# First stage of a cross-attention and expert kernel: products from f16 halves, halves and norm rows on GpSimd, another order within a step

## What is computed

```python
x = x + _L0_xattn_ref(ctx_1024, _layernorm(x, axis=-1), w_q, w_kv, w_out, b_out)   # 16 heads of 16
x = x + _L0_ffn_ref(_layernorm(x, axis=-1), gate_w, gate_b, expert_w, expert_b)    # all 8 experts, weighted by top-2 counts
x = x + _L1_xattn_ref(_layernorm(x, axis=-1), ctx_1024, ctx_1024, mask)
x = x + _L1_ffn_ref(_layernorm(x, axis=-1), W1, b1, W2, b2, Wg, bg)                # top-2 routing
```

## Time and profile before

| | us |
|---|---|
| median of 3 executions | 1119.98 |
| the three | 1128.83, 1119.98, 1119.82 |
| profiled execution | 1129.09 |
| its span, first to last instruction | 1127.3 |
| busy in the span: TensorE | 1004.8 (89%) |
| VectorE | 788.8 (70%) |
| ScalarE | 545.1 (48%) |
| GpSimd | 448.9 (40%) |

### The profile page before, as it was taken

How to read it: one execution, slowest core, us unless ns; L and a number is a source line. 1 busy time by engine, 2 the same in 40 slices (tenths; PEclk the granted TensorE clock), 3 DMA queues, 4 the chain that set the end, 5 groups by cost and what they waited for, 6 DMA issues and landing times. The chain is left out here.

```text
span 1127.3 us, 30896 instructions
## 1 busy us (share of the span) xinstructions
PE 1004.8 (89%) x10536; PEld 709.5 (63%) x10536; DVE 788.8 (70%) x2287; ACT 545.1 (48%) x1087; POOL 448.9 (40%) x648
## 2 busy tenths in 40 slices
PE   3789999999999999987499999999987399999994
PEld 2456666666666666655256666666654288888873
DVE  4377777888777788874377888888875355666553
ACT  1266666666666666655214333334433054555541
POOL 5222222222222222200015666666665525555554
PEclk9699999999999999998699999999986599999998
DMA  4444344343434434310345555555552235555443
GB/s 124 129 125 128 109 127 122 112 128 112 123 115 121 127 109 126 99 59 3 115 145 152 170 180 181 176 178 167 172 175 87 95 83 89 99 97 97 82 70 44
DMA packets 104586, 133.92 MB, mean 119 GB/s; under 512 B 23680, under 2 KB 93776, under 8 KB 104272
## 3 DMA queue, kind: packets, MB, share of 16 engines
q1 hardware_dynamic: 90898, 113.86, 34.0%
q0 software_dynamic: 13536, 18.10, 9.1%
HBM read 93.78 MB, written 38.68 MB: 118 GB/s over the span
## 5 line engine op out<-in xcount | busy, mean ns | idle before, releaser
L631 DVE TENSOR_REDUCE smax<-psum 112x2 f32<-112x750 f32 x256 | 236.7, 936 | 59.3 <-PE psum L355 59.3
L539 ACT ACTIVATE probsT<-psum 125x896 f32<-125x896 f32 x192 | 175.9, 916 | 45.0 <-PE psum L370 44.9
L1487 POOL DMA_INDIRECT out_dram<-y,token_at x70 | 112.1, 1602 | 111.3 <-DMA out_dram<-y,token_at 56.2
L1568 ACT ACTIVATE h<-psum,b 128x256 f32<-128x256 f32 x140 | 58.7, 470 | 99.4 <-PE psum L1515 86.2
L390 PE MATMUL psum<-probsT,v_aug 125*32 125x112 f32 x3072 | 96.6, 268 | 0.0
L288 POOL TENSOR_SCALAR ln_var<-ln_mv 112x1 f32<-112x1 f32 x32 | 7.1, 221 | 208.3 <-DVE ln_mv L643 208.3
L296 POOL TENSOR_TENSOR ctx_lo<-ctxT,ctx_hi 128x750 f16<-128x750 f32 x32 | 51.5, 1611 | 90.6 <-ACT ctx_hi L546 90.6
L355 PE MATMUL psum<-k_stack,q_stack 63*128 63x375 f16 x512 | 84.5, 329 | 1.8 <-DVE smax L631 1.5
L1244 DVE SCALAR_TENSOR_TENSOR acc<-psum,neg_bias,acc 128x448 f32<-128x448 f32 x112 | 75.9, 680 | 11.4 <-PE psum L1063 10.9
L1039 POOL DMA_INDIRECT dispatch_dram<-rows,slots_at x64 | 64.1, 1002 | 46.7 <-DVE slots_at L1347 35.5
L370 PE MATMUL psum<-q_stack,k_stack 64*128 64x112 f16 x1536 | 71.0, 211 | 10.7 <-ACT probsT L539 7.6
(11 more groups left out here) (215 smaller groups left out, 2420.9 us busy)
## 6 DMA issues: line engine op xcount, KB each, us to landing
ctxT<-in_ctxT_dram SPq DMA_DIRECT2D x64, 375.0 KB, 3.7
k_stack<-k_hi_dram SPq DMA_DIRECT2D x64, 188.0 KB, 2.7
ctx_rows<-in_ctx_dram SPq DMA_DIRECT2D x32, 375.0 KB
rows_e<-dispatch_dram SPq DMA_DIRECT2D x70, 136.0 KB
w_raw<-in_w_dram SPq DMA_DIRECT2D x32, 256.0 KB
k_hi_dram<-k_hi SPq DMA_DIRECT2D x32, 188.0 KB, 2.1
k_lo_dram<-k_lo SPq DMA_DIRECT2D x32, 188.0 KB, 2.0
k_stack<-k_lo_dram SPq DMA_DIRECT2D x32, 188.0 KB, 2.8
```

What stands on the lines that cost most here:

```text
L539: nc.scalar.activation(probsT[:, p, c, hg, :, :, :].rearrange("p k h q -> p k (h q)"), psum[0:KC, 0:2, 0:4 * S], ACT.Exp, scale=float(HD) ...
L631: nc.vector.reduce_max(smax[:, (u - LAG_B) % 2, 2 * (s % 4) + s // 4::PAIRS], psum[0:S, pair_bank(s):pair_bank(s) + 2, 0:KV], AX.X).then_i ...
L1487: nc.gpsimd.indirect_dma_start(dram["out"], bass.IndirectOffsetOnAxis(token_at[:, n % 2, s:s + 1], 0), y[:, n % 2, s, :], None, compute_op ...
L1568: nc.scalar.activation(h[:, c, :], psum[:, 1 + c // 2, (c % 2) * TILE:(c % 2 + 1) * TILE], ACT.Relu, bias=b1[:, c, bass.ds(e, 1)]).then_in ...
```

## The change

It does six things, all in `attention_phase`:
1. The query product and the output product are made of f16 halves, three passes each. That needs halves of wq and wo (made once), and xnT_hi, xnT_lo and onT_hi, onT_lo per step: ScalarE writes the upper half from PSUM, VectorE subtracts it (xnT_lo, onT_lo).
2. ScalarE copies queries and keys from PSUM to SBUF once, in f32 (q_full, k_full, in the space of the early weights, called `early`). GpSimd makes q_hi, q_lo, k_hi, k_lo from there. TensorE waits for the copy only.
3. The norm rows xn and x1n are written by GpSimd.
4. On TensorE and ScalarE, `vals((0, 1))` of the new row come before the output product, scores 6 and 7 and `vals((2,))` before unit 4, and the sixth unit just before the queries; `values(2)` comes after the gate.
5. The upper halves of the weights are cast by ScalarE at the start.
6. Semaphores follow.

```diff
--- before.py
+++ after.py
-    wq = sb("wq", [128, DC, D], F32)
-    wk = sb("wk", [128, DC, D], F32)
+    early = sb("early", [128, 2, DC * D], F32)
+    wq, wk = (early[:, n, :].rearrange("p (c d) -> p c d", c=DC) for n in range(2))
+    after = early[:].rearrange("p n w -> p (n w)")
+    k_full = after[:, 0:DC * KV].rearrange("p (c n) -> p c n", c=DC)
+    q_full = after[:, DC * KV:DC * KV + DC * S].rearrange("p (c s) -> p c s", c=DC)
...
+            def ln1_rows_of(t, u):
+
+                xb = x_res[:, bass.ds(t * UNROLL + u, 1), :].rearrange("p o d -> p (o d)")
+                wait(pool, m["ln1_rs"], count(t, u, 1, 1))
+                wait(pool, m["xnT_done"], count(t, u - 1, 1, 1))
+                nc.gpsimd.tensor_scalar(xn[:], xb, ln1_mv[:, 0:1], ln1_rstd[:], ALU.subtract, ALU.mult).then_inc(m["xn_ready"], 1)
...
             ln1_rstd_of(0, 0)
+            ln1_rows_of(0, 0)
             ctx_low(0, 0)
...
+                if on[0]:
+                    wait(pool, m["qfull_ready"], count(t, u, 1, 1))
+                    wait(pool, m["q_out"], count(t, u - 2, 32, 32))
+                    nc.gpsimd.tensor_copy(q_hi[:, u % 2, :, 0:S], q_full[:]).then_inc(m["qhi_ready"], 1)
+                    wait(pool, m["qhi_ready"], count(t, u, 1, 1))
+                    nc.gpsimd.tensor_tensor(q_lo[:, u % 2, :, 0:S], q_full[:], q_hi[:, u % 2, :, 0:S], ALU.subtract).then_inc(m["qlo_ready"], 1)
                 if more:
                     ctx_low(t, u + 1)
+                if on[0]:
+                    for mc in range(DC):
+                        wait(pool, m["kfull_ready"], count(t, u, 2, mc + 1))
...
+                        nc.gpsimd.tensor_copy(k_hi[:, u % 2, mc, 0:KV], k_full[:, mc, :]).then_inc(m["khi_ready"], 1)
+                        wait(pool, m["khi_ready"], count(t, u, 2, mc + 1))
+                        nc.gpsimd.tensor_tensor(k_lo[:, u % 2, mc, 0:KV], k_full[:, mc, :], k_hi[:, u % 2, mc, 0:KV],
+                                                ALU.subtract).then_inc(m["klo_ready"], 1)
                 if more:
                     ln1_rstd_of(t, u + 1)
+                    ln1_rows_of(t, u + 1)
...
+                    wait(pool, m["x1nT_done"], count(t, u - LAG_D - 1, 1, 1))
+                    nc.gpsimd.tensor_scalar(x1n[:], x1, ln2_mv[:, 0:1], ln2_rstd[:], ALU.subtract, ALU.mult).then_inc(m["x1n_ready"], 1)
...
                         wait(pe, m["ctxlo_ready"], count(t, u, 1, 1))
-                        wait(pe, m["qlo_ready"], count(t, u, 1, 1))
+                        wait(pe, m["qfull_ready"], count(t, u, 1, 1))
                     else:
-                        wait(pe, m["klo_ready"], count(t, u, 2, 1))
+                        wait(pe, m["kfull_ready"], count(t, u, 2, 1))
...
+                if not a:
+                    last_unit()
...
                 if a:
+                    last_unit()
                     wait(pe, m["v_ready"], count(t, u - 1, 2, 1))
-                    wait(pe, m["xnT_ready"], count(t, u, 1, 1))
+                    wait(pe, m["xnTlo_ready"], count(t, u, 1, 1))
...
+                        for w, x in ((wq_hi, xnT_hi), (wq_hi, xnT_lo), (wq_lo, xnT_hi)):
...
                 pair_scores(0)
-                if d:
-                    values(2)
...
                 if d:
+                    values(2)
                     values(3)
...
                 pair_scores(5)
+                if a:
+                    vals((0, 1))
                 if d:
-                    wait(pe, m["onT_ready"], count(t, u - LAG_D, 1, 1))
-                    for kc in range(DC):
-                        last = nc.tensor.matmul(bank_d[0:S, 0:D], onT[:, kc, :], wo[:, kc, :], start=(kc == 0), stop=(kc == DC - 1))
+                    wait(pe, m["onTlo_ready"], count(t, u - LAG_D, 1, 1))
...
+                    for x, w in ((onT_hi, wo_hi), (onT_lo, wo_hi), (onT_hi, wo_lo)):
...
                 unit_scoresT(3)
-                if a:
-                    vals((0, 1))
                 pair_scores(6)
+                pair_scores(7)
+                if a:
+                    vals((2,))
                 unit_scoresT(4)
-                if a:
-                    vals((2,))
-                pair_scores(7)
...
+            nc.scalar.activation(wq_hi[:], wq[:], ACT.Copy).then_inc(m["weight_split"], 1)
+            act.wait_ge(m["wkv_in"], 32)
+            nc.scalar.activation(wk_hi[:], wk[:], ACT.Copy).then_inc(m["weight_split"], 1)
+            nc.scalar.activation(wv_hi[:], wv[:], ACT.Copy).then_inc(m["weight_split"], 1)
...
-                    if mc == 0:
-                        wait(act, m["k_out"], count(t, u - 2, 32, 32))
-                    nc.scalar.activation(k_hi[:, u % 2, mc, 0:KV], bank_a[:, 0:KV], ACT.Copy).then_inc(m["khi_ready"], 1)
+                    wait(act, m["klo_ready"], count(t, u - 1, 2, mc + 1))
+                    nc.scalar.activation(k_full[:, mc, :], bank_a[:, 0:KV], ACT.Copy).then_inc(m["kfull_ready"], 1)
...
+                if d and a:
+                    exps(t, u - LAG_D, 5)
...
                 unit_exp(2)
+                if a:
+                    vout((0, 1))
                 unit_exp(3)
                 if a:
-                    vout((0, 1))
+                    vout((2,))
                 unit_exp(4)
-                if a:
-                    vout((2,))
...
+                if a:
+                    wait(dve, m["xnT_ready"], count(t, u, 1, 1))
+                    wait(dve, m["q_done"], count(t, u - 1, 1, 1))
+                    nc.vector.tensor_tensor(xnT_lo[:, :, :].rearrange("p c s -> p (c s)"), psum[:, 3, 0:DC * S],
+                                            xnT_hi[:, :, :].rearrange("p c s -> p (c s)"), ALU.subtract).then_inc(m["xnTlo_ready"], 1)
...
-                klo(0)
...
                 pair_max(4)
-                klo(1)
+                if d:
+                    wait(dve, m["onT_ready"], count(t, u - LAG_D, 1, 1))
+                    wait(dve, m["out_done"], count(t, u - LAG_D - 1, 1, 1))
+                    nc.vector.tensor_tensor(onT_lo[:, :, :].rearrange("p c s -> p (c s)"), bank_d[:, 0:DC * S],
+                                            onT_hi[:, :, :].rearrange("p c s -> p (c s)"), ALU.subtract).then_inc(m["onTlo_ready"], 1)
...
-                if more:
-                    ln1_out(t, u + 1)
                 pair_max(7)
-                if d:
-                    wait(dve, m["ln2_rs"], count(t, u - LAG_D, 1, 1))
-                    wait(dve, m["x1nT_done"], count(t, u - LAG_D - 1, 1, 1))
-                    nc.vector.tensor_scalar(x1n[:], x1, ln2_mv[:, 0:1], ln2_rstd[:], ALU.subtract, ALU.mult).then_inc(m["x1n_ready"], 1)
```

More of the change, by code:

```diff
@@ L136, in attention_phase @@
     o_nat = sb("o_nat", [S, D], F32)
-    onT = sb("onT", [128, DC, S], F32)
+    onT_hi, onT_lo = sb("onT_hi", [128, DC, S], F16), sb("onT_lo", [128, DC, S], F16)
     ln2_stats = sb("ln2_stats", [S, 6], F32)
@@ L579, in step @@
                     negate_maxima()
-                if d:
+                if d and not a:
                     exps(t, u - LAG_D, 5)
```

98 lines of the change are left out of this document (54 added, 44 removed).

## The result

The changed kernel takes 1137.49 us (median of 4 executions, 1134.97 to 1142.01), the kernel before on the same chip 1124.4 us (1119.82 to 1131.87). The ratio is 1.0116, 95% interval 1.0075 to 1.0157. The forecast was 1088.9 us; the change is slower by about 1%.

A forecast was written before the change was run, and what follows sets the result against it. TensorE's row of instructions was taken to set the 15.13 us step. Savings less one new wait gave 1.04 us per step, 29.1 over 28 steps, plus 2 at the start: 31.1, so 1119.98 becomes 1088.9 us, range 1078 to 1108.

The forecast's parts named there:

- the price of xn and x1n on GpSimd: Norm rows written by GpSimd: 0.47 us each, in 4.8 us of added GpSimd work per step, 8.8 in all.
- the new wait for maximum 6: TensorE's transposes of xn need the bank that maximum 6 on VectorE still uses: 0.15 us lost per step.
- Query product, 0.27: TensorE's query product as twelve f16 passes takes 0.72 us instead of 0.99: 0.27 saved per step, bounds nothing and 0.40.
- Output product, 0.31: TensorE's output product as six f16 matmuls takes 0.65 us instead of 0.96: 0.31 saved per step, bounds 0.24 and 0.35.
- Waits for k_lo and onT, and for exponentials: TensorE's waits per step in the first stage: 0.18 us saved for k_lo, 0.23 for onT, 0.20 for exponentials.
- My walk: One step traced with old slots in the new order: xn and x1n from GpSimd in time by less than 0.2 us.
- smaller gain: Rival, chance 0.22: 1098 to 1108 us, one or two terms failing: query weight loads, GpSimd casts at two-input price, SyncE's queue.
- no change: Rival, chance 0.08: within 11 us; a new wait, such as a late x1n, takes all, needing 1.04 us lateness per step.
- VectorE, 10.2 us a step: VectorE loses k_lo, q_lo, xn and x1n, gains xnT_lo and onT_lo: from 12.1 to 10.2 us per step.
- Start: 2 us forecast: First steps: moving the cast of wk gains nothing; a shorter chain of product, copy, k_lo in steps 1 to 3 saves 2 us.
- Tail: put at nothing: Steps without queries: no gain or loss, since ScalarE's chain rules and onT_lo costs what the shorter product gives.
- SyncE's queue, the rival for slower: Rival, chance 0.04: about 1134 us; SyncE's queue decides beyond its slack of 1.58 us per step, as GpSimd's halves come later.

The follow-up runs named there:

- the run with the cheap pair: Changed kernel with xn and x1n on GpSimd made by (mult, add) with constants instead of (subtract, mult), leaving the normalisation out: step 14.41 us, 1108.94 us, one run.

## Why the prediction was wrong

Two steps of it failed: the price of xn and x1n on GpSimd, taken as 0.47 us from a row with another pair of operations, where it is 1.24; and the new wait for maximum 6, put at 0.15 us a step. Of the 1.22 us between the forecast step (14.09) and the measured one (15.31), the run with the cheap pair gives back 0.90; the rest, 0.32, is there with cheap rows too.

*Query product, 0.27: right.* Twelve passes take 0.69 us (252.74 to 253.43), forecast 0.72. An estimate by the 81 ns of the Trainium skill (TensorE: Matmul & The Clock Gate, Back-to-back issue gap) would have been 0.97. This trace doesn't bear it out: 0.058 us a pass. Undone, the product cost 0.38, since its f32 slot was then 1.08 and not 0.99.

*Output product, 0.31: mostly right.* 0.75 us (262.02 to 262.77) for 0.65, so 0.21 saved of 0.31. With the wait for an exponential that the forecast read into the same slot, 1.05 became 0.75: 0.30 of the 0.40 forecast for both.

*Waits for k_lo and onT, and for exponentials: right.* The first two left the list, the third fell from 24.0 us over 26 steps to 11.7 over 24.

*The sum of the savings: right, in part by luck.* Without the waits in front of the two turns the step is 14.13 us, and without the one for maximum 3 as well 13.85, so 1.28 us were saved where the forecast had 1.19 before its new wait. The rest was not foreseen: the last two values groups, now side by side behind the gate, take 1.29 us where they took 0.71 + 0.72 with the gate between (0.14 saved), and the turn of x1n takes 0.34 for 0.19 now that a transposed unit follows it (0.15 lost).

*GpSimd: the step that failed.* The halves were priced well (0.50, 0.87, 0.37 and 0.58 for 0.52, 0.90, 0.40 and 0.61). For xn and x1n I took the mask's (mult, add) row as the nearest, and called the two-input price, 0.67, a bound from above. It is none. The price hangs on the pair of operations, and no row of before had (subtract, mult) on GpSimd; "like the nearest one-input row" was a choice, 2.6 times too low. Nor do the forecast's own prices lie on one line: with 0.52 for 375 elements and 0.40 for 224, a row of 256 would have been 0.43, not 0.47; that is small beside the rest. My walk had both rows in time by less than 0.2 us, so 0.77 us more for each, one behind the other, reached TensorE's waits; with the cheap pair (0.40 us, and constants) 0.90 us of the step come back, 28 x 0.9 = 25 us. The rival "smaller gain" had the mechanism, with each row some 0.4 late and 11 us for both; GpSimd came to 10.0 us a step for 8.8; "no change" said that GpSimd would have to be 1 us slower over three instructions, and it was 1.5 slower over two.

*Wait for maximum 6, 0.15: right in kind, mis-sized.* Behind cheap rows it costs 0.37 us, and with xn on VectorE behind maximum 6 it costs 0.66. So even with the price for GpSimd that the forecast had, the step would have been 14.4 us, and 28 x 0.3 = 8 us of the forecast were never there; with the rows on VectorE it is 14.73, and 28 x 0.63 = 18 us of the forecast are missing.

*VectorE, 10.2 us a step: 10.9.* One small operation did most of it: the cast of two indices, 159 ns before, 698 ns now (84 to 476 us, before and after):

```profile
L711 DVE CAST chosen_at<-top_at 112x2 f32<-112x2 uint32 x26 | 4.1, 159 | 0.0
```

```profile
L758 DVE CAST chosen_at<-top_at 112x2 f32<-112x2 uint32 x26 | 18.1, 698 | 0.0
```

It runs while GpSimd makes k_lo (258.15 to 258.87, k_lo from 257.95 to 258.85). The prediction said that the added GpSimd work would hurt only if VectorE kept such operations, and that the ones it saw leave; I had looked only at those. The price is not only busy time: the 0.28 us a step of scores 5 for maximum 3 stand behind this cast, a term that the sum didn't have. At the start wq_lo takes 1603 ns beside GpSimd's ctx_lo, and wk_lo, of the same size, 691 beside a memset. By the rule of exclusive port use in the Trainium skill (SBUF — State Buffer, Who interferes with whom) that is what to expect, and the trace agrees; the cast, with a single small input, is one more case of it.

*Start: 2 us forecast.* Measured against the period it is 28 x 0.18 = 5.0 lost and 2.5 lost in all up to the last query product, so 2.5 gained.

*Tail: put at nothing, 6.7 us lost, by the order and by the clock.* I looked at the sum of the work there and not at the order. The gate, now ahead of `values(2)`, meets xT_lo 0.4 to 0.9 us before it is there, and onT_lo stands behind maximum 4 with no values projection to cover it. The price of the second, about 0.5 without cover, was in the prediction; that the steps without queries have no cover was overlooked. From the last query product to the end of the stage it is 70.7 us before and 77.4 after, and the runs lead from one to the other: 1.2 go with xn and x1n on GpSimd (77.4 for 76.2), 2.7 with the order (76.2 for 73.5), both pairs at a clock of 0.77 to 0.78; 4.9 with the clock (73.5 at 0.77 for 68.6 at 0.87); and 2.1 are saved (68.6 for 70.7 before, at 0.85). These are single executions. So the fault in the order is worth about 3 us. The clock of the last steps, which no term of the sum held, accounts for some 4 of the 6.7 by my estimate (4.9 us for a difference of 0.10, and 0.85 before against 0.77 after).

*SyncE's queue, the rival for slower: not it.* Its wait for neg_max, the slack, is 35.6 us over 24 steps, 1.5 each, about as before.

Together: 33.6 us missed up to the last query product (31.1 forecast, 2.5 lost), 6.7 in the tail, 1.8 gained in the rest: 38.5, the difference between the forecast for the profiled execution, 1098.0, and 1136.56.
